# One chip kernel, three attentions: row maxima turned in two groups of heads a batch instead of four

## What is computed

```python
h = _ln(x) * (1 + sc_msa) + sh_msa
h = _self_attn(h, w_qkv, b_qkv, w_so, b_so)      # windows of 128 tokens, rolled by 64
x = x + h * g_msa
h = _ln(x) * (1 + sc_mca) + sh_mca
h = _topk_cross_attn(h, context, ...)            # softmax over the 16 largest of 256 scores
x = x + h * g_mca
h = _ln(x) * (1 + sc_mlp) + sh_mlp
h = _swiglu(h, w_m1, b_m1, w_m2, b_m2)           # hidden width 1024
x = x + h * g_mlp
# then the second layer:
xq, xkv = _ada_ln(x, t_vec, ...), _ada_ln(ctx, t_vec, ...)
scores = einsum('bqhd,bkhd->bhqk', q, k) / sqrt(16)
out = einsum('bhqk,bkhd->bqhd', softmax(scores), v)
return x + (out @ Wp + bp)
```

## Time and profile before

| | |
|---|---|
| median of three runs | 1281.58 us |
| the profiled execution | 1281.51 us |
| its span, first to last instruction | 1279.6 us |
| TensorE busy | 1197.1 us (94%), 13710 products |
| VectorE busy | 1128.0 us (88%) |
| ScalarE busy | 1035.5 us (81%) |
| GpSimd busy | 852.7 us (67%) |
| mean granted TensorE clock | 0.988 of full speed |

### The profile page before, as it was taken

One profiled execution on the slowest core, in us unless ns is written; L12 is line 12 of the kernel. 1 busy time (PEld: TensorE's weight loads), 2 busy tenths in 40 slices (PEclk: granted clock), 3 DMA queues, 4 the chain that ended last, 5 costly groups with the idle time before them and its releaser, 6 DMA issues. The chain is left out here.

```text
span 1279.6 us, 39100 instructions
## 1 busy us (share of the span) xinstructions
PE 1197.1 (94%) x13710; PEld 850.3 (66%) x13710; DVE 1128.0 (88%) x3808; ACT 1035.5 (81%) x2193; POOL 852.7 (67%) x1134
## 2 busy tenths in 40 slices
PE   7778898999999999999999999999999999989887
PEld 6665566667676776767676766767676766656654
DVE  3579999899999999999999999999999999988443
ACT  3745688889897979889897989889797979776864
POOL 1315597959586877868686877968596877857310
PEclk9989999999999999999999999999999999999999
DMA  7531021211111121212021121212021121110111
GB/s 200 157 81 43 23 76 34 61 38 45 48 50 54 47 64 27 55 44 73 27 68 44 47 64 52 51 27 64 15 81 30 47 56 42 28 27 2 43 35 34
DMA packets 111392, 67.27 MB, mean 53 GB/s; under 512 B 13836, under 2 KB 107870, under 8 KB 111198
## 3 DMA queue, kind: packets, MB, share of 16 engines
q1 hardware_dynamic: 109166, 63.71, 18.8%
q10 hardware_dynamic: 2032, 1.05, 0.5%
HBM read 22.33 MB, written 4.19 MB: 21 GB/s over the span
## 5 line engine op out<-in xcount | busy, mean ns | idle before, releaser
L1246 ACT ACTIVATE prob<-turned_score 128x1024 f32<-128x1024 f32 x320 | 325.7, 1018 | 82.8 <-PE turned_score L908 81.2
L1521 POOL TENSOR_TENSOR pair<-full,pair 128x512 f16<-128x512 f32 x182 | 210.6, 1162 | 112.8 <-ACT pair L1201 106.6
L1405 DVE MATCH_REPLACE8 rest<-top,score 128x256 f32<-128x256 f32 x512 | 208.2, 415 | 0.0
L1419 DVE MATCH_REPLACE8 far<-best,rest 128x256 bf16<-128x256 f32 x512 | 205.7, 409 | 0.5 <-issue 0.5
L1402 DVE MAX8 top<-score 128x8 f32<-128x256 f32 x512 | 193.4, 419 | 10.7 <-PE score L908 10.3
L1527 POOL TENSOR_SCALAR far<-far 128x512 bf16<-128x512 bf16 x256 | 158.6, 620 | 61.9 <-DVE far L1419 42.6
L1392 DVE TENSOR_REDUCE rowmax_l<-score 128x4 f32<-128x1024 f32 x121 | 147.6, 1220 | 30.5 <-issue 19.8
L908 PE MATMUL work<-pair_n,w_m_hi 128*128 128x256 f16 x1024 | 173.6, 273 | 0.3 <-issue 0.3
L908 PE MATMUL work<-pair_n,w_m_lo 128*128 128x256 f16 x512 | 139.5, 273 | 0.0
L1201 ACT ACTIVATE pair<-full 128x512 f16<-128x512 f32 x192 | 121.0, 630 | 18.0 <-ACT full L1194 0.7
L908 PEld LDWEIGHTS work<-pair_n,w_m_hi 128*128 128x128 f16 x1024 | 96.2, 98 | 20.0 <-issue 9.5
(11 more groups left out here) (212 smaller groups left out, 3191.0 us busy)
## 6 DMA issues: line engine op xcount, KB each, us to landing
k_stack_t<-pair SPq DMA_DIRECT2D x96, 64.0 KB, 2.5
k_stack_l<-pair SPq DMA_DIRECT2D x96, 64.0 KB, 2.6
q_stack_w<-pair SPq DMA_DIRECT2D x93, 64.0 KB, 2.6
k_stack_w<-pair SPq DMA_DIRECT2D x93, 64.0 KB, 2.6
q_stack_t<-pair SPq DMA_DIRECT2D x93, 64.0 KB, 2.6
q_stack_l<-pair SPq DMA_DIRECT2D x93, 64.0 KB, 2.6
ctx_t<-in_ctx_turned SPq DMA_DIRECT2D x16, 256.0 KB, 2.9
ctx_l<-in_ctx SPq DMA_DIRECT2D x16, 256.0 KB, 2.8
```

The lines of the kernel that those rows point to most:

```text
L1246: act.activation(prob[:, at:at + 2, :], both_b[:, :, :], ACT.Exp).then_inc(exp_done, 1)
L1405: m = dve.match_replace(rest[p % 2][:, t, :], eight[:, t, :], bank[:, t * L:(t + 1) * L], -FAR)
L1419: m = dve.match_replace(far[p % NFAR][:, t, :], best[p % 2][:, t, :], rest[p % 2][:, t, :], -FAR)
L1521: pool.tensor_tensor(pr[:, 1, :, :], whole[:, :, :], pr[:, 0, :, :], ALU.subtract).then_inc(split_lo, 1)
```

## The change

The window attention takes two guard groups a batch instead of four in batches 1 to 15, and the last attention in batches 0 to 14. The first w batch, the last l batch and the whole top-k attention keep four. A group of w or l then holds 8 heads: its maxima fill 16 columns of rowmax, are turned by one product to 16x128, copied by one instruction and transferred as 4 KB. A b step waits for the group that holds its heads (w: b 0 and 1 for group 0, 2 and 3 for group 1; l: four b steps a group). 30 gd, gc and gg of w and 30 of l go. Guard tiles and rowmax grow to 32 rows and columns.

All five order strings are written anew. The TensorE list has 1579 steps instead of 1639, ScalarE's 1175 instead of 1235, SyncE's 373 steps become 313; VectorE's 889 and GpSimd's 733 steps are the same ones in another order. The weight loads come in a slightly different order at the start, and the products of no use are 528 in other places. The middle of TensorE's list, one batch long, begins like this (first before, then after):

The core of the diff:

```diff
+GUARDS = {"w": 2, "t": 4, "l": 2}
+EDGE_GUARDS = {("w", 0): 4, ("l", 15): 4}
+
+
+def groups(s, b):
+
+    return EDGE_GUARDS.get((s, b), GUARDS[s])
+
+
+def guard_no(s, b, g):
+
+    return sum(groups(s, one) for one in range(b)) + g
...
-        rowmax = {s: [sb(f"rowmax_{s}{i}", [P, 8], F32) for i in range(2)] for s in "wl"}
-        guard = {s: [sb(f"guard_{s}{i}", [8, P], F16) for i in range(2)] for s in "wtl"}
+        rowmax = {s: [sb(f"rowmax_{s}{i}", [P, 2 * H], F32) for i in range(2)] for s in "wl"}
+        guard = {s: [sb(f"guard_{s}{i}", [2 * H, P], F16) for i in range(2)] for s in "wtl"}
...
                 elif kind == "gg":
-                    n = NG * b + i
+                    n, many = guard_no(s, b, i), H // 2 // groups(s, b)
...
-                    sp.dma_start(stack[s][b % NS[s]]["q"][NR:64 + NR + 1:64, 2 * i:2 * i + 2, :],
-                                 guard[s][n % 2][:, :]).then_inc(guard_in[s], 16)
+                    sp.dma_start(stack[s][b % NS[s]]["q"][NR:64 + NR + 1:64, many * i:many * (i + 1), :],
+                                 guard[s][n % 2][0:4 * many, :]).then_inc(guard_in[s], 16)
...
                 elif kind == "gd":
-                    n = NG * b + i
-                    pe.wait_ge(a_free, a_unit(s, b, 2 * i + 1 if s == "w" else 4 * i + 3))
+                    n, rows = guard_no(s, b, i), 2 * H // groups(s, b)
+                    pe.wait_ge(a_free, a_unit(s, b, (8 if s == "w" else 16) // groups(s, b) * (i + 1) - 1))
...
-                    turn(d_take(piece, b, i)[0:8, 0:P], src).then_inc(d_ready, 1)
+                    turn(d_take(piece, b, i)[0:rows, 0:P], src).then_inc(d_ready, 1)
                 elif kind == "b":
...
-                    pe.wait_ge(guard_in[s], 16 * (NG * b + (i if s == "w" else i // 2) + 1))
+                    pe.wait_ge(guard_in[s], 16 * (guard_no(s, b, i * groups(s, b) // (4 if s == "w" else 8)) + 1))
...
-                    act.activation(guard[s][n % 2][:, :], d_bank("gd_" + s, b, i)[0:8, 0:P], ACT.Copy,
+                    act.activation(guard[s][n % 2][0:rows, :], d_bank("gd_" + s, b, i)[0:rows, 0:P], ACT.Copy,
                                    scale=-1.0).then_inc(guard_out[s], 1)
...
                 elif kind == "rm":
-                    n = NG * b + (i if s == "w" else i // 2)
+                    each = (4 if s == "w" else 8) // groups(s, b)
+                    n, half = guard_no(s, b, i // each), H // groups(s, b)
```

More of the change, by code:

```diff
@@ L54 @@
 BY_TWO = {"wk": 0, "wq": 0, "tq": 0, "lq": 15}
+GUARDS = {"w": 2, "t": 4, "l": 2}
[4 more added lines that the diff above has]
+    return sum(groups(s, one) for one in range(b)) + g
 ORDERS = {
     "pe": (
[1 row of a table removed]
[1 row of a table added]
         "gd_w:0:2 a_w:0:3 b_w:0:1 o_w:0 gd_w:0:3 o_w:0:1 b_w:0:2 o_w:0:2 b_w:0:3 x4_n1:1 o_w:0:3 ot_w:0 bk_w:0 "
[127 rows of a table removed]
-    "act": (
[100 rows of a table removed]
-    "dve": (
[70 rows of a table removed]
-    "pool": (
[88 rows of a table removed]
-}
-IDLE_WORK = ("pj_wq:0:0=59 a_w:0:0=6 gd_w:0:0=22 gd_w:0:1=19 gd_w:0:2=11 bk_w:0:0=17 x4_n2:0:0=25 pj_tq:0:0=38 "
-             "a_w:1:0=13 a_t:0:0=20 b_w:1:0=28 o_w:1:0=8 a_t:0:2=9 a_t:0:5=61 x4_n2:1:0=14 b_t:0:4=16 a_t:1:0=11 "
-             "pr_w:2:0=12 x4_n4:14:0=5 o_l:13:2=12 ot_l:13:0=10 bk_l:13:0=8 m2:15:2=11 x4_n4:15:0=5 pj_lq:15:0=19 "
-             "a_l:15:7=12 bk_l:15:0=14 pr_l:15:0=33")
[121 rows of a table added]
+    "act": (
[94 rows of a table added]
+    "dve": (
[70 rows of a table added]
+    "pool": (
[83 rows of a table added]
+}
+IDLE_WORK = ("pj_wq:0:0=59 a_w:0:0=28 gd_w:0:1=20 gd_w:0:2=12 bk_w:0:0=17 x4_n2:0:0=25 pj_tq:0:0=39 a_w:1:0=7 "
+             "a_t:0:0=20 b_w:1:0=5 b_w:1:2=38 gd_t:0:0=5 bk_w:1:0=29 a_t:0:4=18 b_t:0:4=32 gd_t:0:3=18 a_w:2:1=17 "
+             "bk_t:0:0=5 pr_w:2:0=28 bk_l:13:0=5 xt_m:15:0=6 pj_lq:15:0=23 gd_l:14:1=18 o_l:14:3=7 bk_l:15:0=14 "
+             "pr_l:15:0=33")
 def idle_work():
@@ L757, in unit, with guard_before @@
             return i // 2, i % 2
+        def guard_before(n, s):
+            b = max(one for one in range(B) if guard_no(s, one, 0) <= n)
+            return d_no["gd_" + s, b, n - guard_no(s, b, 0)]
         def heads(g):
@@ L1012, in _ @@
                     else:
-                        src = rowmax[s][n % 2][:, :]
-                    turn(d_take(piece, b, i)[0:8, 0:P], src).then_inc(d_ready, 1)
+                        src = rowmax[s][n % 2][:, 0:rows]
+                    turn(d_take(piece, b, i)[0:rows, 0:P], src).then_inc(d_ready, 1)
                 elif kind == "b":
@@ L1377, in _ @@
                 elif kind == "rm":
-                    n = NG * b + (i if s == "w" else i // 2)
+                    each = (4 if s == "w" else 8) // groups(s, b)
+                    n, half = guard_no(s, b, i // each), H // groups(s, b)
                     if (s, b, i) not in by_bank_no:
                         dve.wait_ge(a_ready, a_no["a_" + s, b, i])
-                    if n >= 2 and (s == "w" or i % 2 == 0):
-                        dve.wait_ge(d_ready, d_no["gd_" + s, (n - 2) // NG, (n - 2) % NG])
-                    at, wide, of = (0, 4, P) if s == "w" else (2 * (i % 2), 2, L)
+                    if n >= 2 and i % each == 0:
+                        dve.wait_ge(d_ready, guard_before(n - 2, s))
+                    at, wide, of = (4 * (i % each), 4, P) if s == "w" else (2 * (i % each), 2, L)
                     if (s, b, i) in by_bank_no:
@@ L1388, in _ @@
                                 dve.wait_ge(a_ready, a_no["a_" + s, b, i])
-                            dve.tensor_reduce(rowmax[s][n % 2][:, 4 * z + at:4 * z + at + wide],
+                            dve.tensor_reduce(rowmax[s][n % 2][:, half * z + at:half * z + at + wide],
                                               bank_a[z].rearrange("p (h k) -> p h k", k=of), AX.X, ALU.max).then_inc(a_free, 1)
                         continue
-                    dve.tensor_reduce(rowmax[s][n % 2][:, :].rearrange("p (z m) -> p z m", z=2)[:, :, at:at + wide],
+                    dve.tensor_reduce(rowmax[s][n % 2][:, 0:2 * half].rearrange("p (z m) -> p z m", z=2)[:, :, at:at + wide],
                                       both_a[:, :, :].rearrange("p z (h k) -> p z h k", k=of), AX.X,
```

6 lines of the change are left out of this document (3 added, 3 removed), and 753 rows, old and new, of the table ORDERS.

## The result

The changed kernel takes 1300.36 us (1299.46 to 1305.43) beside 1282.62 us for the kernel before on the same chip: a ratio of 1.0152, 95% interval 1.0132 to 1.0171 (the two medians alone give 1.0138). Forecast was 1278.6 us in a range of 1272 to 1287. The profiled execution ran 1300.87 us, its span is 1299.1 us, 19.5 us more than before.

What follows compares the result with a forecast made beforehand. VectorE was taken to bound the ramp, TensorE the long middle (with 2 us of waits a period), chains the tail. From 1281.58 us, -4.7 (TensorE) + 2 (b steps) - 0.3 (tail) = -3.0 gave 1278.6 us, range 1272 to 1287.

Steps and rivals of the forecast that it cites:

- A long middle set by TensorE: From 300 to 1100 us TensorE, busy 786.2 of 800 us, sets the time, with 2 us of waits a period.
- Minus 4.7 us on TensorE: 60 turnings fewer at 0.11 us, 6.6 us, less 1.5 for shape changes and 0.4 lost in the ramp.
- The changes of shape: 15 more changes of array shape between TensorE steps, at 0.10 us each: +1.5 us.
- Plus 2 us given back: At b steps, closer together after the change, waiting for the previous b's exponential: 2 us taken, under half of 4.7.
- ScalarE and SyncE at nothing: 60 guard copies (9.6 us of ScalarE) and 60 guard transfers on SyncE removed, both costed at nothing, being covered.
- the cover of 11 us of TensorE work: First a step comes 11 us or more of TensorE work after its projections, so SyncE's queue has time to spare.
- Ramp and tail: VectorE stays the ramp's bound; tail between -1.5 and +1.5 us, taken as -0.3.
- The ramp slips: Rival: new load order delays first batches by 1 to 3 us, 1281 to 1283 us; 0.28 shared with given back.
- Given back: Rival: crowding of b steps costs its full 4.7 us, 1281.3 us; 0.28 shared with a slipped ramp.
- b steps queue: Rival: in batches 3 to 13, 32 close b pairs each stall 0.35 us more on exponentials, +4.2, 1285.8 us; 0.30.
- The turning at full length: Rival: each of 60 turnings frees its whole 0.272 us on TensorE, 16.3 us, 1265 us or so; 0.01.
- My last sentence: If the middle's period grows while named waits stay, the loss is in row maxima or work banks, the reasoning wrong.

Runs made afterwards that it cites:

- run 15: Kernel before, with 60 turnings of the window and last attentions issued twice on TensorE alone, nothing moved: 1286.1 us, ratio 1.0030.
- run 9: Kernel before in its order, with 60 turnings, copies and transfers left out and nothing moved or waiting longer: 1281.5 us, ratio 1.0000.
- run 2: Order of the kernel before, only the window attention in two groups (batches 3 to 15), eight b steps moved back: 1287.5 us, ratio 1.0049.
- run 8: Changed kernel, same order, each of the 60 merged turnings, copies and transfers issued as two halves at the same place: 1315.0 us, ratio 1.0253.
- run 13: Kernel before, with 90 VectorE reductions of the window and last attentions reading only half of each row's keys: 1283.7 us, ratio 1.0012.
- run 14: Kernel before with the edits of run 9 and run 13 together: 1278.1 us, ratio 0.9971.
- run 10: Changed kernel and order, but merged turnings wait only for the first four of their eight heads' maxima: 1299.6 us, ratio 1.0133.
- run 5: Changed kernel's code and tiles, with the order strings of the kernel before and four groups everywhere: 1282.5 us, ratio 1.0000.
- run 16: Changed kernel, with 90 VectorE reductions reading only half of each row's keys: 1300.0 us, ratio 1.0137.
- run 17: Changed kernel, with 100 ScalarE exponentials of the merged attentions covering only half their columns: 1299.4 us, ratio 1.0145.
- run 6: Changed kernel, with 43 TensorE steps that waited over 0.3 us each put behind the independent step that followed: 1321.2 us, ratio 1.0304.
- run 11: Changed kernel, with the order of the kernel before up to 210 us on every engine: 1298.7 us, ratio 1.0126.
- run 18: Kernel before, order and four groups kept, with 86 ScalarE exponentials covering only half their columns: 1281.9 us, ratio 1.0013.
- run 4: Order of the kernel before, window (batches 3 to 15) and last attention (0 to 12) in two groups, b steps moved back: 1326.5 us, ratio 1.0339.
- run 3: Order of the kernel before, window in two groups (batches 3 to 15), last attention in three (0 to 12): 1292.2 us, ratio 1.0085.
- run 7: Kernel before, with 20 TensorE steps that waited each put behind the independent step that followed: 1295.4 us, ratio 1.0106.
- run 12: Kernel before, with 20 swaps of neighbouring independent TensorE steps at places where neither waited: 1293.0 us, ratio 1.0078.

## Why the prediction was wrong

*What bounds the middle.* "A long middle set by TensorE" was half of it. Run 15 bears it out (0.40 of 0.44 us a batch when turnings are added), run 9 doesn't (0.08 of 0.44 when they go). The 2 us of waits a period that I had noted were part of what bounds the middle: they grew when work was taken out (runs 2 and 9).

*Minus 4.7 us on TensorE: the step that failed first.* The price of a turning in the list, 0.11 us, is right: pairs of turnings in run 8 and the whole of run 15 show it. A turning of 16 columns is listed with 273 to 277 ns, hardly more than the 272 of before. What failed is the next sentence, that 6.6 us less work are 6.6 us less path. Nothing moved, nothing added, it was 0.1 us with an interval of 2.6 us to either side (run 9: 0.9980 to 1.0021). With VectorE's reductions cut as well the same 60 were worth 5.6 us (runs 13 and 14), so what they bring may hang on what else is short, though the middle shows little of it there. The changes of shape were priced right, too: TensorE's own work a batch fell by 0.35 us, where four turnings are 0.44 and one change of shape is 0.10.

*Plus 2 us given back: the step that failed most.* I looked for the price of the new lists in two pairs of steps, turning to b and b to b. Both were fine, as the waits for guards (none) and exponentials (2.0 us) show. The list was rewritten everywhere, though, and the hand-overs that lost their distance were others: o to ot, ot to bk, bk to pr, maxima to the turnings of top-k. Waits of over 0.45 us went from 7.2 to 30.2 us, and the middle lost 14.6 us net where I had -4.7 + 2 = -2.7. Run 10 shows that it is the order and not the waiting for eight heads, run 5 that it isn't the code or the tiles, and runs 16 and 17 that it isn't VectorE's or ScalarE's load. That the distances at these hand-overs are the cause inside the order is read from the traces; putting distance back was tried once, in TensorE's list alone (run 6), and made it worse.

*ScalarE and SyncE at nothing.* ScalarE's 9.6 us less bought nothing, as said. SyncE at nothing holds for what was taken away. But the cover of 11 us of TensorE work that I counted for the projections' transfers isn't all slack: copies, six issues and the landing fill it. In the kernel before the first top-k score of batch 7 stands at 546.08 us, and the last transfer for it landed at 546.03. In the new order the waits of top-k's scores for these transfers grew from 0.2 to 1.8 us between 300 and 1100 us, a term that I didn't have. Whether the issues are free when added, run 8 doesn't show.

*Ramp and tail.* The ramp slips: right in kind, 7.2 us by the first copy in one profiled execution. Part of that is chance: in the profiled executions of runs 5, 9, 13, 15 and 18, which have the old order, that copy lies anywhere from 305.0 to 312.2 us. The old start gave 1.7 us at the median (run 11). VectorE between 100 and 200 us is 97.07 us busy, under the 99 that I had asked for, and the granted clock is 0.95 in place of 1.00 there, 0.85 in place of 0.90 in the first 100 us: more of TensorE's start at 1.2 GHz. The tail gained 2.3 us, against -1.5 to +1.5.

*The rivals.* "Given back" and "b steps queue" named the sign of the result in one case, but their mechanism isn't there: b's waits fell. The turning at full length is out (runs 9 and 15). My last sentence, that a longer period with these waits unchanged would make the reasoning wrong, is what happened, though the loss is in neither of the two places it names: TensorE's waits for the row maxima of w and l in the middle went from 1.2 to 1.6 us, those for a work bank not yet emptied from about 0.6 to 1.2 us.

*What stays open.* Whether two groups of l force such an order, or a better one exists. Run 4 says that l's first b steps can't simply move back in the old list (+44 us), run 3 that three groups cost 0.7 us a period, run 2 that w alone is free and brings nothing. Runs 6, 7 and 12 show that swapping pairs in TensorE's list alone isn't the way; swapping them in all lists, or a new search of the whole order, wasn't tried. Nor is it shown what holds the old order's period at 71.4 us when any one engine has less to do, nor how much of that is single late transfers, as at two places of run 9. No version here that computes everything beats the kernel before.

## What to carry to other kernels

Where TensorE, VectorE and ScalarE run interleaved from hand-written lists at 88% and more of the middle, an instruction taken out need not be worth its length: 60 of them were worth nothing here. Try that first by leaving them out without moving anything. Price a rewritten order by all its hand-overs, for each pair of producer and consumer the work that stands between, and not only those that the change is about. A wait that keeps its length to hundredths when the engine it names gets less to do points to distance in the list, not to that engine's load.

## What had not been expected of the hardware

The run-to-run repeatability of single waits, 0.01 us after 800 us of five engines' interleaved work (runs 10, 16 and 17), and first scores of a batch within 0.45 us between two kernels with other addresses, from batch 4 of w to the end of the middle (run 5). How dear a place in TensorE's list is when the other lists stay: 0.5 to 0.7 us for a swap of neighbours that costs nothing by their lengths, from 83 swaps in three runs. And single issues on SyncE's queue of 0.75 to 2.2 us where nearly all take 0.6, 26 to 40 a trace behind 200 us, for which nothing here shows a reason.
